# Moving a chunk's four row normalizations on ScalarE from positions 54–57 to 50–53 of a bidirectional Mamba kernel

## The chip, the cores and the metric

One core of a Trainium2 chip runs the whole program. The metric is the device time of one launch in microseconds. The kernel before was run three times; the median was 7565.02 us.

The engines are called as in the profile: PE (TensorE), DVE (VectorE), ACT (ScalarE), POOL (GpSimd) and SP (SyncE, which issues nearly all DMAs).

## The reference

The input is x, two sequences of 4096 rows of 512. The reference is a block with adaptive layer norms:

```
h = layernorm(x) * (1 + ca) + sa
x = x + ga * bidirectional_mamba(h)          # inner width 1024, 16 states per channel
h = layernorm(x) * (1 + cb) + sb
x = x + gb * fp6_quantized_linear(h)
```

The Mamba block projects h to u and z, runs a causal convolution of 4 taps and a SiLU over u, forms delta (a softplus), B and C from u, and then for each of 1024 channels and 16 states runs the recurrence

```
state[t] = exp(delta[t] * A) * state[t-1] + delta[t] * u[t] * B[t]
y[t]     = sum over the 16 states of state[t] * C[t]
```

followed by y + u*Dp, the gate silu(z), and an output projection. It runs once forwards and once backwards in time.

## The kernel before

The program has three parts: a short setup, the scan (from about 219 us to 7117 us of the profiled span), and a final stage with the second norm and the quantized linear. The change touches the scan alone.

The scan treats 32 chunks of 512 time steps: 16 forwards, 16 backwards. A chunk has 8 tiles of 128 channels (`MT`), and a tile has 16 states. Two states make one position, so a tile has 8 positions (`NQ`) and a chunk 64 (`POS`, p = 0 to 63). Every engine runs its own program, written out position by position, and they meet in semaphores. At each position:

- POOL multiplies B by delta*u for both states (`dBu`, L689). It works up to four pairs ahead of DVE. States 3, 4, 7 and 11 (`ASIDE`) are also multiplied by C on POOL (L698, tile `hR`), at the 6th position of the tile for 3 and 4, the 7th for 7 and the 8th for 11. Each of these waits until ACT has copied the last column of the state out of `hR` (L814, `aside_saved`), since the product overwrites it. At the 7th position POOL also makes delta and delta*u of the next tile (L672, L676).
- ACT makes exp(delta*A) for both states (L803) into a ring of four places in PSUM (`scans`), each free again when DVE has used the state from four before. Between these come its other duties: it empties PSUM banks (L740 the convolution into u, L751 z, L770 turned states, L759 B and C, L785 y), keeps states (L814), and at eight positions of the chunk (`GATED`) it switches to the SiLU table (L918), applies SiLU to u (L746) and z (L755), and switches back (L924).
- DVE runs the recurrence as a scan over 512 columns (L1160) and multiplies the other states by C (L1176, `hC`).
- PE adds the products up in PSUM (L1025) and does all projections, transposes and convolutions of this and the next chunk as background work (`SCHEDULE`).

Seven of the eight switches to SiLU stand at the last position of a tile (p = 7, 15, 23, 31, 39, 47, 63). The one of the seventh tile stands at p = 52, in the tile's middle, and does SiLU for two u tiles and z.

Rows of x for the chunk after the next are loaded into the first half of `comb` (`xin`) soon after p = 19 and are normalized in place by four ACT instructions of 128x512 (`normalize`, L791), one at each of the four positions from `NORM_POS` on, after the position's other duties and before its switch of tables if it has one. PE transposes them at p = 58, 60, 61 and 62 (`H0` to `H3`) and waits there for all four (`ln_done`).

Of the kernel before, what the change touches and what calls it, by code (L numbers as in the profile page):

```python
# [116 lines left out]
assert all(LAST[name][0][0] != "Y" for name in LAST if LAST[name][1])  # L117

RING = 2
NORM_POS = 54  # L120

# [234 lines left out]
def scan_stage(nc, io, dram):  # L358

    with ExitStack() as ctx:  # L360
# [345 lines left out]
        def _(act):  # L706
# [81 lines left out]
            def normalize(c, tt, table):  # L788
                if tt == 0:
                    act.wait_ge(x_loaded, c * (16 * TT) + 16 * TT)  # L790
                act.activation(xin[:, tt, :], xin[:, tt, :], ACT.Identity, scale=table[:, C_ROWS + tt:C_ROWS + tt + 1],  # L791
                               bias=table[:, C_ROWS + TT + tt:C_ROWS + TT + tt + 1]).then_inc(ln_done, 1)
# [59 lines left out]
            for i in range(CHUNKS):  # L852
# [4 lines left out]
                for j in range(MT):  # L857
# [3 lines left out]
                    for q in range(NQ):  # L861
# [52 lines left out]
                        for tt in range(TT):  # L914
                            if p == NORM_POS + tt:
                                normalize(i + 2, tt, cur)
# [709 lines left out]
```

## Time and profile before

| | us |
|---|---|
| median of three runs | 7565.02 |
| lowest and highest | 7552.77, 7570.42 |
| the profiled execution, its own time | 7552.77 |
| its span, first to last instruction | 7550.9 |
| PE, DVE, ACT, POOL busy in the span | 6864.3, 6824.4, 6159.4, 6964.4 |
| mean granted TensorE clock | 0.967 |

The busy times are sums over the whole span, setup and final stage included. Instructions on one engine overlap by some tens of nanoseconds, so what one costs in a queue is the distance between starts, not its duration. In a row of the timeline the bracket at the end gives the idle time before the instruction and who ended it; "issue" means that the profile shows no releaser.

### The profile page before, as it was taken

Reading aid. Unit: us, or ns where it says so; the run is one execution under the profiler, and the core shown is the slowest. Engines: PE = TensorE matmul, PEld = TensorE weight load, DVE = VectorE, ACT = ScalarE, POOL = GpSimd, SP = SyncE. Lnnn points to the kernel's source line nnn. Section 1 sums busy time; section 2 is a strip of 40 time slices with the busy share of each in tenths; the row PEclk is TensorE's granted clock in tenths of the full one; section 3 lists DMA queues with packets and bytes.
Section 4 is the critical chain, followed back from the end, with each engine's and each line's share of the span. In section 5 each row is a group of like instructions: output and inputs, shape, how many; then the busy total and the mean of one; then the engine's idle time right before and its main releaser. Section 6 shows DMA issues by size and latency. Waiting matters only on the chain. (4 is left out here: it accounts for less than half of the span.)

```text
span 7550.9 us, 110015 instructions
## 1 busy us (share of the span) xinstructions
PE 6864.3 (91%) x32682; PEld 4082.2 (54%) x32682; DVE 6824.4 (90%) x9069; ACT 6159.4 (82%) x12569; POOL 6964.4 (92%) x3774
## 2 busy tenths in 40 slices
PE   6899999999999999999999999999999999999889
PEld 3455555555555555555555555555555555555455
DVE  2799999999999999999999999999999999999766
ACT  1788888888888888888888888888888888888645
POOL 0899999999999999999999999999999999999678
PEclk8999999999999999999999999999999999999999
DMA  7544455444444454444444544444445444444555
GB/s 255 148 137 130 129 147 149 107 142 140 137 133 129 141 149 109 140 137 136 133 130 143 150 108 141 140 138 134 128 139 149 110 140 140 138 132 130 153 191 173
DMA packets 605392, 1064.01 MB, mean 141 GB/s; under 512 B 113584, under 2 KB 221872, under 8 KB 596336
## 3 DMA queue, kind: packets, MB, share of 16 engines
q1 hardware_dynamic: 602704, 1055.84, 47.7%
q8 instruction: 261, 4.28, 0.2%
q14 instruction: 347, 2.84, 0.1%
q10 hardware_dynamic: 2080, 1.05, 0.0%
HBM read 926.61 MB, written 130.05 MB: 140 GB/s over the span
## 5 line engine op out<-in xcount | busy, mean ns | idle before, releaser
L689 POOL TENSOR_TENSOR dBu<-Bb,du 128x1024 f32<-128x1024 f32 x2048 | 4784.6, 2365 | 1.9 <-DMA Bb<-bc_scratch 1.8
L1160 DVE TENSOR_TENSOR_SCAN scans<-scans,state,dBu 128x512 f32<-128x512 f32 x2304 | 2904.0, 1281 | 480.8 <-ACT scans L803 308.6
L803 ACT ACTIVATE scans<-delta,A 128x512 f32<-128x512 f32 x4096 | 2752.9, 693 | 356.0 <-DVE hC L1176 321.7
L1025 PE MATMUL yT<-ident,hC 128*128 128x128 f32 x9216 | 1411.7, 284 | 252.3 <-DVE hC L1176 250.0
L1176 DVE TENSOR_TENSOR hC<-scans,Cb 128x512 f32<-128x512 f32 x2304 | 1558.8, 682 | 0.0
L698 POOL TENSOR_TENSOR hR<-hR,Cb 128x512 f32<-128x512 f32 x1024 | 1293.7, 1275 | 220.8 <-ACT state L814 219.2
L1025 PEld LDWEIGHTS yT<-ident,hC 128*128 128x128 f32 x9216 | 1085.3, 145 | 654.0 <-DVE hC L1176 353.8
L1160 DVE TENSOR_TENSOR_SCAN hR<-scans,state,dBu 128x512 f32<-128x512 f32 x1024 | 1294.8, 1264 | 0.0
L1018 PE MATMUL bg<-u,comb 128*128 128x512 f32 x2112 | 989.1, 594 | 0.9 <-DVE u L1133 0.9
L1160 DVE TENSOR_TENSOR_SCAN hV<-scans,state,dBu 128x512 f32<-128x512 f32 x768 | 969.4, 1262 | 16.9 <-ACT scans L803 12.6
L957 PE MATMUL bg<-hT,win_u 128*128 128x512 f32 x2112 | 967.9, 599 | 0.9 <-ACT hT L725 0.9
L979 PE MATMUL bg<-hT,win_z 128*128 128x512 f32 x2048 | 963.5, 593 | 0.0
L770 ACT ACTIVATE turned<-bg,CT 128x128 f32<-128x128 f32 x3072 | 865.3, 365 | 42.1 <-PE bg L1002 38.2
L1025 PEld LDWEIGHTS yT<-ident,hR 128*128 128x128 f32 x4096 | 504.0, 151 | 363.3 <-issue 280.7
L1025 PE MATMUL yT<-ident,hR 128*128 128x128 f32 x4096 | 638.9, 293 | 59.9 <-POOL hR L698 59.9
L957 PEld LDWEIGHTS bg<-hT,win_u 128*128 128x128 f32 x2112 | 382.7, 191 | 445.0 <-issue 441.8
L1002 PEld LDWEIGHTS bg<-ident,hV 128*128 128x128 f32 x3072 | 374.7, 143 | 394.1 <-issue 254.3
L1018 PEld LDWEIGHTS bg<-u,comb 128*128 128x128 f32 x2112 | 368.6, 190 | 330.9 <-issue 323.4
L979 PEld LDWEIGHTS bg<-hT,win_z 128*128 128x128 f32 x2048 | 359.4, 191 | 306.0 <-issue 306.0
L1002 PE MATMUL bg<-ident,hV 128*128 128x128 f32 x3072 | 477.6, 279 | 50.8 <-DVE u L1133 30.0
L972 PE MATMUL bg<-comb,wtap 128*32 128x512 f32 x2080 | 299.3, 647 | 219.6 <-DMA comb<-pre_scratch 218.1
L1036 PEld LDWEIGHTS bg<-ident,turned 128*128 128x128 f32 x3084 | 366.5, 145 | 156.2 <-issue 156.2
(163 smaller groups left out, 7574.1 us busy)
## 6 DMA issues: line engine op xcount, KB each, us to landing
comb<-pre_scratch SPq DMA_DIRECT2D x1040, 256.0 KB, 4.6
Bb<-bc_scratch SPq DMA_DIRECT2D x264, 512.0 KB, 7.9
Cb<-bc_scratch SPq DMA_DIRECT2D x264, 512.0 KB, 8.6
win_u<-in_win SPq DMA_DIRECT2D x264, 256.0 KB, 4.7
pre_scratch<-pre SPq DMA_DIRECT2D x264, 256.0 KB, 3.8
comb<-comb_scratch SPq DMA_DIRECT2D x66, 1024.0 KB, 8.8
win_z<-in_win SPq DMA_DIRECT2D x257, 256.0 KB, 2.8
part_scratch<-pre SPq DMA_DIRECT2D x132, 256.0 KB, 2.0
```

Source lines behind the costliest of these rows:

```text
L689: pool.tensor_tensor(dBu[:, q % AHEAD], Bb[:, 2 * q:2 * q + 2, :], du[:, j % 2, :].unsqueeze(1).broadcast_to([P, 2, T]), ALU.mult).then_in ...
L698: pool.tensor_tensor(hR[:, k, :], hR[:, k, :], Cb[:, n, :], ALU.mult).then_inc(hR_made, 1)
L770: ins = act.mul(turned[:, TURNED.index(n), tt * P:(tt + 1) * P], bank[:, tt * P:(tt + 1) * P], CT[:, s, tt, n:n + 1])
L803: act.activation(place(n)[:], delta[:, j % 2, :], ACT.Exp, scale=A[:, i % 2, j * N + n:j * N + n + 1]).then_inc(dA_made, 1)
L957: ins = nc.tensor.matmul(bank[:], win_u[:, m % RING, k, :], hT[:, slot, k, :], start=(k == 0), stop=(k == KD - 1))
L979: ins = nc.tensor.matmul(bank[:], win_z[:, j % 2, k, :], hT[:, slot, k, :], start=(k == 0), stop=(k == KD - 1))
L1002: ins = nc.tensor.matmul(bank[:, tt * P:(tt + 1) * P], hV[:, TURNED.index(n), tt * P:(tt + 1) * P], ident[:], start=True, stop=True, is_tr ...
L1018: ins = nc.tensor.matmul(bank[:], comb[:, m, tt * P:(tt + 1) * P], u[:, s, m, :], start=(k == 0), stop=(k == MT - 1))
L1025: ins = nc.tensor.matmul(yT[:, tt * P:(tt + 1) * P], product[:, tt * P:(tt + 1) * P], ident[:], start=first and tt == 0, stop=False, is_tr ...
L1036: nc.tensor.matmul(bank[:, tt * P:(tt + 1) * P], turned[:, k, tt * P:(tt + 1) * P], ident[:], start=False, stop=False, is_transpose=True, ...
L1160: nc.vector.tensor_tensor_scan(to, place(n)[:], dBu[:, q % AHEAD, k, :], state[:, c:c + 1], ALU.mult, ALU.add).then_inc(h_made, 1)
L1176: nc.vector.tensor_tensor(hC[:, (j * NS + STRAIGHT.index(n)) % HC, :], bank[:], Cb[:, n, :], ALU.mult).then_inc(hC_made, 1)
```

## The change

One number: the position from which the four normalizations are issued.

```diff
-NORM_POS = 54
+NORM_POS = 50
```

It is read in one place, in ACT's loop over positions, `if p == NORM_POS + tt: normalize(i + 2, tt, cur)`. The programs of PE, DVE, POOL and SP are the same, instruction for instruction. On ACT two places differ, once in each of the 32 chunks.

ACT in the first chunk before, from the evacuation of the last convolution (p = 50) to the switch to SiLU (p = 52). L803 is the exponential, L721 the softplus's logarithm, L770 a turned state, L814 the copy of kept states, L751 z.

```order
L740 ACTIVATE u<-bg,bconv 128x512
L803 ACTIVATE scans<-delta,A 128x512
L721 ACTIVATE sp_a<-sp_a 128x512
L803 ACTIVATE scans<-delta,A 128x512
L770 ACTIVATE turned<-bg,CT 128x128 x4
L803 ACTIVATE scans<-delta,A 128x512
L814 COPY state<-hR 128x2
L751 COPY z<-bg 128x512
L803 ACTIVATE scans<-delta,A 128x512
L918 ACT_TABLE_LOAD
```

The same place in the changed kernel, where the last row here stands right ahead of the switch:

```order
L740 ACTIVATE u<-bg,bconv 128x512
L791 ACTIVATE comb<-comb,cur 128x512
L803 ACTIVATE scans<-delta,A 128x512
L721 ACTIVATE sp_a<-sp_a 128x512
L803 ACTIVATE scans<-delta,A 128x512
L770 ACTIVATE turned<-bg,CT 128x128 x4
L791 ACTIVATE comb<-comb,cur 128x512
L803 ACTIVATE scans<-delta,A 128x512
L814 COPY state<-hR 128x2
L751 COPY z<-bg 128x512
L803 ACTIVATE scans<-delta,A 128x512
L791 ACTIVATE comb<-comb,cur 128x512
```

Three L791 now stand ahead of the switch, one of them ahead of the copy L814 128x2 and two ahead of z.

The second place is on ACT too, from the return to the exponential's table (p = 52) to p = 55, before. The L814 128x1 at its head is the copy of state 7, the one at its end that of state 11.

```order
L924 ACT_TABLE_LOAD
L803 ACTIVATE scans<-delta,A 128x512 x2
L814 COPY state<-hR 128x1
L883 ACTIVATE state<-state,cur 128x16
L770 ACTIVATE turned<-bg,CT 128x128 x4
L803 ACTIVATE scans<-delta,A 128x512 x2
L814 COPY state<-hV 128x3
L791 ACTIVATE comb<-comb,cur 128x512
L803 ACTIVATE scans<-delta,A 128x512
L770 ACTIVATE turned<-bg,CT 128x128 x4
L803 ACTIVATE scans<-delta,A 128x512
L814 COPY state<-hR 128x1
```

The same in the changed kernel:

```order
L924 ACT_TABLE_LOAD
L803 ACTIVATE scans<-delta,A 128x512 x2
L814 COPY state<-hR 128x1
L883 ACTIVATE state<-state,cur 128x16
L770 ACTIVATE turned<-bg,CT 128x128 x4
L791 ACTIVATE comb<-comb,cur 128x512
L803 ACTIVATE scans<-delta,A 128x512 x2
L814 COPY state<-hV 128x3
L803 ACTIVATE scans<-delta,A 128x512
L770 ACTIVATE turned<-bg,CT 128x128 x4
L803 ACTIVATE scans<-delta,A 128x512
L814 COPY state<-hR 128x1
```

The fourth L791 stands one position earlier than the first one stood before, behind the copy of state 7 and ahead of two exponentials. The three that stood at p = 55, 56 and 57 are gone from there.

## Rows read from the trace of the kernel before

**Rows 1.** page: busy us of each engine, share of span, instructions
```profile
PE 6864.3 (91%) x32682; PEld 4082.2 (54%) x32682; DVE 6824.4 (90%) x9069; ACT 6159.4 (82%) x12569; POOL 6964.4 (92%) x3774
```

**Rows 2.** list of waits, POOL, whole span: us in total, times, longest
```profile
POOL hR L698 <- ACT state L814: 219.2, 162, 3.0
...
POOL dBu L689 <- DMA Bb<-bc_scratch: 1.8, 5, 0.7
```

**Rows 3.** windows: five of the eight tiles of chunk 8 (columns in the first row)
```profile
core 0: us, PE busy (x) PEld busy (x) DVE busy (x) ACT busy (x) POOL busy (x), PEclk, DMA share, GB/s
1940.03:1966.06 26.03, 23.02 (x101) 14.12 (x100) 25.36 (x34) 20.43 (x43) 25.95 (x14) 0.92 0.90 339
1966.06:1993.59 27.53, 27.53 (x131) 16.77 (x130) 26.09 (x34) 22.77 (x47) 26.09 (x15) 1.00 0.10 32
...
2045.81:2074.13 28.32, 26.18 (x137) 15.25 (x136) 26.30 (x35) 25.20 (x53) 26.06 (x15) 1.00 0.65 158
...
2101.49:2128.91 27.42, 23.77 (x128) 13.36 (x129) 24.38 (x33) 25.39 (x47) 26.03 (x14) 1.00 0.41 106
2128.91:2154.96 26.05, 21.10 (x115) 14.12 (x114) 25.84 (x34) 23.05 (x49) 25.97 (x14) 0.95 0.30 86
```

**Rows 4.** timeline of POOL, seventh tile of chunk 8: start us, us, what, [idle before]
```profile
2122.66 2.36 POOL L689 TENSOR_TENSOR dBu<-Bb,du 128x1024 f32<-128x1024 f32 x1
2126.34 1.27 POOL L698 TENSOR_TENSOR hR<-hR,Cb 128x512 f32<-128x512 f32 x1 [1.32 <-ACT state L814]
2127.56 1.28 POOL L672 TENSOR_TENSOR delta<-sp_a,sp_r 128x512 f32<-128x512 f32 x1
```

**Rows 5.** timeline of POOL, the same place in chunks 0 and 31
```profile
403.83 1.26 POOL L698 TENSOR_TENSOR hR<-hR,Cb 128x512 f32<-128x512 f32 x1 [1.31 <-ACT state L814]
...
7081.25 2.50 POOL L698 TENSOR_TENSOR hR<-hR,Cb 128x512 f32<-128x512 f32 x2 [0.35 <-ACT state L814]
...
7087.94 1.27 POOL L698 TENSOR_TENSOR hR<-hR,Cb 128x512 f32<-128x512 f32 x1 [1.89 <-ACT state L814]
```

**Rows 6.** timeline of ACT, chunk 8, positions 50 to 55
```profile
2114.25 0.68 ACT L740 ACTIVATE u<-bg,bconv 128x512 f32<-128x512 f32 x1
2115.99 0.69 ACT L803 ACTIVATE scans<-delta,A 128x512 f32<-128x512 f32 x1 [1.06 <-DVE hC L1176]
...
2119.92 0.72 ACT L803 ACTIVATE scans<-delta,A 128x512 f32<-128x512 f32 x1
2120.66 1.28 ACT L918 ACT_TABLE_LOAD   x1
...
2126.09 0.17 ACT L814 COPY state<-hR 128x1 f32<-128x1 f32 x1
...
2127.38 1.31 ACT L803 ACTIVATE scans<-delta,A 128x512 f32<-128x512 f32 x2
...
2128.69 0.83 ACT L791 ACTIVATE comb<-comb,cur 128x512 f32<-128x512 f32 x1
2129.40 0.68 ACT L803 ACTIVATE scans<-delta,A 128x512 f32<-128x512 f32 x1
```

**Rows 7.** groups of instructions, L791: count | busy us, mean ns | idle
```profile
L791 ACT ACTIVATE comb<-comb,cur 128x512 f32<-128x512 f32 x128 | 105.4, 824 | 0.0
```

**Rows 8.** timeline of DVE, the same stretch
```profile
2125.67 1.29 DVE L1160 TENSOR_TENSOR_SCAN scans<-scans,state,dBu 128x512 f32<-128x512 f32 x1 [1.33 <-ACT scans L803]
...
2128.69 2.46 DVE L1160 TENSOR_TENSOR_SCAN scans<-scans,state,dBu 128x512 f32<-128x512 f32 x2
...
2132.60 2.47 DVE L1160 TENSOR_TENSOR_SCAN scans<-scans,state,dBu 128x512 f32<-128x512 f32 x2 [0.21 <-issue]
```

**Rows 9.** timeline of PE, the same stretch
```profile
2124.39 0.66 PE L1025 MATMUL yT<-ident,hC 128*128 128x128 f32 x4 [1.33 <-DVE hC L1176]
```

**Rows 10.** windows of 3 us around the end of the eighth tile
```profile
2150.00:2153.00 3.00, 1.59 (x12) 1.60 (x13) 3.00 (x5) 3.00 (x10) 3.00 (x3) 0.90 0.01 4
2153.00:2156.00 3.00, 3.00 (x17) 3.00 (x16) 3.00 (x5) 2.77 (x8) 2.92 (x3) 0.54 0.28 59
```

## The prediction

> **What bounds the kernel now.** The page's busy times come first [rows 1]. Four engines are busy for 82 to 92% of the span, POOL most (6964.4 us), ACT least (6159.4 us). Such shares do not say which engine sets the end of a tile, so the next view is POOL's list of waits [rows 2]. In the scan it waits for one thing that matters: the product `hR` times C (L698) waits for ACT's copy of the state (L814), 219.2 us in 162 waits. For the loads of B it waits 1.8 us in all.
>
> The third view is the windows by tile [rows 3]. Each window runs on POOL from the start of one tile's delta*u (L676) to the start of the next, which lies one position and a half before the tile on the other engines. POOL's busy time is 25.95 to 26.09 us in every tile, whatever its length. So a tile lasts 26.0 us of POOL's work plus POOL's waits: 26.05 and 26.03 us in the eighth and the first tile, where it hardly waits, but 28.32 us in the fifth and 27.42 us in the seventh. Whatever makes POOL wait longer adds to the time, and whatever only fills other engines' idle time does not.
>
> The change lies in the seventh and eighth tile, so the fourth view is the timeline there. In chunk 8 POOL finishes its seventh pair at 2122.66 + 2.36 = 2125.02 us, and the product of state 7 starts only at 2126.34 us, 1.32 us idle [rows 4]. What it waited for is ACT's copy of state 7, issued at 2126.09 us, 0.17 us long [rows 6]. That copy stands behind the switch to SiLU at p = 52. This is so in all 32 chunks. There are 47 such waits in the seventh tiles; the first chunk's is 1.31 us and the last chunk's two are 0.35 and 1.89 us [rows 5], and together they make 67.0 us. In no chunk is POOL late enough for ACT to have slack at that copy. Behind the wait POOL runs on without a gap (L672 at 2127.56 us), and DVE, which waits 0.21 us for the pair of the tile's last position [rows 8], goes along with POOL.
>
> **What one normalization costs ACT.** It takes 824 ns in the mean, 128 times [rows 7], but instructions overlap: from the start of one at 2128.69 us to the start of the next instruction at 2129.40 us are 0.71 us [rows 6]. I take 0.71 us for each; the whole duration, 0.83 us, is the upper end.
>
> **The change part by part.** Nothing is added or removed; 4 x 32 = 128 instructions move. They issue no DMA, and no wait is new: the rows of x are loaded from p = 20 on, and `cur` is used at earlier positions already. The queues of SP, PE, DVE and POOL are as before.
>
> - First normalization, p = 50. It comes behind the evacuation of the convolution at 2114.25 us. The next exponential began at 2115.99 us, after ACT sat idle for 1.06 us waiting for DVE [rows 6]. 0.71 us fits into 1.06 us: cost 0. Without that cover it would be 0.71 us.
> - Second, p = 51, and third, p = 52. No idle time stands on ACT between 2115.99 us and the copy of state 7. Before the switch ACT runs into the table load without a gap: the exponential of 2119.92 us ends at 2120.64 us and the load begins at 2120.66 us [rows 6]. So both push the switch, the SiLUs and the copy of state 7 back by 2 x 0.71 = 1.42 us, and POOL, which already waits there, by as much. On the way the copy of states 3 and 4 is late by 0.71 us. A wait for it that this makes, like the 0.35 us of the last chunk, lies inside the 1.42 us, since POOL waits again behind it. DVE's wait for the first exponential after the switch, 1.33 us [rows 8], becomes 2.75 us by the same delay, not a further one. Cost 1.42 us per chunk; 2 x 0.83 = 1.66 us is the upper end.
> - Fourth, p = 53. It stands behind the copy of state 7, so POOL's wait does not see it, but ahead of the exponentials of p = 54. By the clock of the delayed engines these come 0.71 us later: the first ended at about 2127.38 + 0.69 = 2128.07 us, now at 2128.78 us, and DVE wants it at 2128.69 us [rows 6, 8]. That is 0.09 us late, or some 0.2 us with the time from one engine to the other (0.08 us from the end of ACT's copy, 2126.26 us, to POOL's start [rows 4, 6]). DVE has 0.21 us of waiting for POOL three scans later [rows 8]. I take 0; the ends are 0 and 0.71 us.
> - What is gone from p = 54 to 57. ACT saves there what it spent before. In the eighth tile ACT is busy for 23.05 of 26.05 us and in the first tile of the next chunk for 20.43 of 26.03 us, while POOL waits for nearly nothing (26.05 - 25.97 = 0.08 us, and 26.03 - 25.95 = 0.08 us) [rows 3]. The relief falls where ACT binds nobody. I take a gain of 0; the lower end is those 0.16 us per chunk.
>
> Sum: 2 x 0.71 x 32 = 45.4 us more. Against the profiled execution, 7552.8 us, that gives 7598 us. It is the lowest of three runs, 12 us under the median of 7565.0 us; carried to the median the sum is 7610 us, +0.60%. The ends of the terms: -0.16 x 32 = -5 us for the relief, and 0.24 x 32 = +8 us for full durations, 0.71 x 32 = +23 us each for the first and the fourth normalization.
>
> **The rivals.**
>
> *The stall is free.* ACT has 18% of idle time, and work moved about within its queue might find room. The time would stay at 7565 us. For it: ACT is the least busy of the four [rows 1]. Against it: in the 50 us around the change that idle time lies in the eighth and first tile, and the seventh has ACT at 25.39 of 27.42 us [rows 3], with the wait on its copy behind [rows 4]. The Trainium skill (Perfetto Trace Analysis, Identifying Performance Opportunities) says that improving a kernel generally means improving the engine with the highest occupancy. Read alone, that is POOL and not ACT, and the rule would price this change at 0. The rows above disagree for this stretch: POOL's gap ends with ACT. The same section also tells the reader to look at the gaps of that engine and what ends them, which is what was done here.
>
> *Given back in the second tile.* The other side. In the next chunk's second tile POOL's window is 27.53 us against 26.09 us busy, 1.44 us of waiting, and PE is busy in all of it [rows 3]: ACT waits there for PE, and POOL for ACT. If the B and C evacuation and the transposes of x, reached by ACT with three normalizations fewer ahead of them, let PE start the next chunk with less arrears, that wait could go: 1.44 x 32 = 46 us, and 45.4 - 46 = -0.7 us, 7564 us, not slower. It decides from the point where PE has no idle time left between the change and the second tile. Against it: PE idles 26.05 - 21.10 = 4.95 us in the eighth tile and 26.03 - 23.02 = 3.01 us in the first, so it has caught up by then, and starting its work earlier wins nothing.
>
> *More is exposed, or PE's clock falls.* If the first and the fourth normalization cost too, it is 4 x 0.71 x 32 = 90.9 us: 7656 us. Much the same comes from the clock. PE waits 1.33 us for DVE in the seventh tile [rows 9], which becomes 2.75 us. Late in the eighth tile, after PE was busy for 1.59 of 3 us, its granted clock is 0.54, near the lower level of 1.2 GHz [rows 10]. A window of 3 us at half speed loses 1.5 us of PE's work; were that on the chain in each chunk, it would be 48 us on top, 7658 us. Against it: the fourth has DVE's 0.21 us as cover, and PE has 4.95 us of idle time in the eighth tile to make good a fall.
>
> **How the numbers follow.** The forecast has 0.78, the free stall 0.05, the second tile 0.07, the greater cost 0.10. The predicted time is the forecast's, 7610 us; its own range is 7592 to 7635 us, from the ends above and some 8 us for the spread of the three runs. The range of 8 in 10 is 7585 to 7645 us: it takes in the half of the third rival in which one further normalization costs, and leaves out the two at about 7565 us, 0.12 together. A measurement of this kernel can tell 0.2%, 15 us, from no change. Faster by more needs the second tile's wait gone and part of the 45 us hidden: 0.03. Within it: 0.09. Slower: 0.88.
>
> **What would show it.** In the profile after, POOL's wait for L814 in the whole span is about 219 + 45 = 265 us; the seventh tile of chunk 8 lasts 28.8 us and not 27.4, while the other windows keep their lengths; ACT's idle time of 1.06 us before the exponential of p = 51 falls to 0.35 us; DVE's wait after the switch grows from 1.33 to 2.75 us; ACT's idle time in the eighth tile grows. A seventh tile of 27.4 us would make the forecast wrong in its main step. A second tile shorter than 27 us would show the second rival, and a seventh tile over 29.5 us, or a lengthened eighth, the third.

## The result and the profile after

The changed kernel is slower: 7640.28 us in the median of 4 runs (7634.85 to 7645.27) against 7561.79 us before. The ratio is 1.0104 with a 95% interval from 1.0087 to 1.0121, so about 78 us (66 to 91) were lost. The profiled execution of the changed kernel took 7615.2 us, with a span of 7613.5 us, and is faster than the median of its timed runs by some 25 us; its windows by tile show the smaller loss of about 62 us. The mean granted TensorE clock was 0.967 in the profile before and is 0.963 in this one, 0.959 to 0.961 in the four timed runs.

First the tiles of chunk 8 after, the columns as in [rows 3]: window, length, busy time of PE, PEld, DVE, ACT and POOL, PE's granted clock, and DMA.

```profile
1956.92:1983.17 26.25, 22.18 (x92) 13.60 (x91) 24.87 (x34) 20.30 (x42) 25.97 (x14) 0.87 0.88 327
1983.17:2011.08 27.91, 27.91 (x132) 16.91 (x131) 26.21 (x34) 22.74 (x47) 26.04 (x15) 1.00 0.11 32
...
2063.25:2091.27 28.02, 26.07 (x137) 15.16 (x136) 26.40 (x35) 25.02 (x53) 26.02 (x14) 1.00 0.65 161
...
2118.63:2148.80 30.17, 26.19 (x129) 15.42 (x130) 24.26 (x33) 27.50 (x49) 26.07 (x15) 0.89 0.38 97
2148.80:2175.30 26.50, 22.39 (x123) 14.81 (x122) 26.50 (x34) 20.87 (x48) 26.02 (x14) 0.94 0.32 92
```

These are the first, second, fifth, seventh and eighth tile. POOL is still busy for 26.0 us in each. The seventh grew from 27.42 to 30.17 us; some of this is chunk 8's own, since the mean over all 32 chunks went from 28.23 to 29.78 us. But the eighth has 26.50 us and not 26.05, the first 26.25 and not 26.03, and the second 27.91 and not 27.53. PE's clock over the first tile is 0.87, where it was 0.92.

Now ACT in the seventh tile after, answering to [rows 6]: start, duration, instruction, and in brackets the idle time before it.

```profile
2133.17 0.69 ACT L740 ACTIVATE u<-bg,bconv 128x512 f32<-128x512 f32 x1
2133.74 0.81 ACT L791 ACTIVATE comb<-comb,cur 128x512 f32<-128x512 f32 x1
2134.45 0.69 ACT L803 ACTIVATE scans<-delta,A 128x512 f32<-128x512 f32 x1
...
2137.19 0.84 ACT L791 ACTIVATE comb<-comb,cur 128x512 f32<-128x512 f32 x1
...
2139.69 0.83 ACT L791 ACTIVATE comb<-comb,cur 128x512 f32<-128x512 f32 x1
2140.55 1.28 ACT L918 ACT_TABLE_LOAD   x1
...
2145.97 0.17 ACT L814 COPY state<-hR 128x1 f32<-128x1 f32 x1
```

The first L791 follows the evacuation of 2133.17 us at once. In this chunk the exponential behind it has no idle time left ahead of it; in 19 of 32 chunks some 0.16 to 0.36 us are left of what was about 1 us. Two more L791 stand ahead of the table load. From the L791 of 2137.19 to the copy of state 7 at 2145.97 us ACT has no gap. Next POOL and DVE at that place, answering to [rows 4] and [rows 8]:

```profile
2138.80 2.50 POOL L698 TENSOR_TENSOR hR<-hR,Cb 128x512 f32<-128x512 f32 x2 [1.42 <-ACT state L814]
2141.26 2.36 POOL L689 TENSOR_TENSOR dBu<-Bb,du 128x1024 f32<-128x1024 f32 x1
2146.22 1.26 POOL L698 TENSOR_TENSOR hR<-hR,Cb 128x512 f32<-128x512 f32 x1 [2.60 <-ACT state L814]
```

```profile
2145.55 1.29 DVE L1160 TENSOR_TENSOR_SCAN scans<-scans,state,dBu 128x512 f32<-128x512 f32 x1 [2.81 <-ACT scans L803]
```

POOL's wait for the copy of state 7 is 2.60 us, and a wait of 1.42 us for the copy of states 3 and 4 stands ahead of it. DVE's wait for the exponential behind the switch went from 1.33 to 2.81 us. In the list of waits over the whole span (total, times, longest) these three answer to [rows 2] and to the forecast of 265 us for POOL's:

```profile
DVE scans L1160 <- ACT scans L803: 371.3, 246, 119.9
...
POOL hR L698 <- ACT state L814: 278.0, 211, 2.8
...
PE bg L1002 <- ACT turned L770: 66.8, 33, 2.2
```

POOL's was 219.2 us before. DVE's was 308.6 us and PE's wait for the turned state 20.3 us. DVE's longest, 119.9 us, is a single one that the kernel before has too (118.9 us). Inside the 32 seventh windows POOL's waits for this copy went from 67.0 to 115.4 us and DVE's for the exponentials from 71.4 to 127.3 us.

The last views show what the forecast did not contain: PE and its clock in the eighth tile and at the turn of the chunk. First PE's timeline, then windows of 3 us with the clock in the column before DMA's two, then ACT.

```profile
2147.43 0.66 PE L1002 MATMUL bg<-ident,hV 128*128 128x128 f32 x4 [2.11 <-ACT turned L770]
...
2156.85 1.92 PE L1031 MATMUL bg<-u,skip 128*128 128x512 f32 x2
2158.55 2.21 PE L1036 MATMUL bg<-ident,turned 128*128 128x128 f32 x12
...
2161.13 1.12 PE L1007 MATMUL bg<-dbc,wdt 32*128 32x512 f32 x2
```

```profile
2154.00:2157.00 3.00, 1.73 (x13) 1.26 (x11) 3.00 (x5) 0.69 (x1) 3.00 (x2) 0.94 0.00 0
2157.00:2160.00 3.00, 3.00 (x10) 1.86 (x9) 3.00 (x5) 1.91 (x4) 3.00 (x2) 0.50 0.00 0
2178.00:2181.00 3.00, 1.38 (x8) 0.75 (x8) 2.02 (x2) 2.96 (x4) 3.00 (x3) 0.92 1.01 384
2181.00:2184.00 3.00, 1.92 (x9) 1.92 (x10) 3.00 (x6) 1.87 (x3) 3.00 (x2) 0.50 1.02 415
2184.00:2187.00 3.00, 3.00 (x10) 1.86 (x9) 3.00 (x5) 2.42 (x4) 3.00 (x2) 0.50 1.03 418
```

```profile
2162.34 0.69 ACT L712 ACTIVATE sp_r<-bg,bdt 128x512 f32<-128x512 f32 x1 [1.77 <-issue]
```

The same instructions of chunk 8 in the kernel before:

```profile
2136.86 1.02 PE L1031 MATMUL bg<-u,skip 128*128 128x512 f32 x2
...
2139.56 1.12 PE L1007 MATMUL bg<-dbc,wdt 32*128 32x512 f32 x2
```

```profile
2140.76 0.69 ACT L712 ACTIVATE sp_r<-bg,bdt 128x512 f32<-128x512 f32 x1
```

PE waits 2.11 us at 2147.43 us. From 2157 us, at the head of the eighth tile, the granted clock is 0.50, that is 1.2 of 2.4 GHz, and the two instructions of the skip matmul (L1031) take 1.92 us where they took 1.02. Behind them comes the projection for the next delta (L1007), which starts 4.28 us after L1031 and not 2.70. ACT reads it in L712, and stood idle for 1.77 us before that. The profile names no releaser for this wait, but in both kernels L712 begins 0.08 to 0.09 us after L1007 has ended. In the mean over the 32 chunks ACT is idle for 1.06 us ahead of this L712, against 0.38 us before. The next fall is at 2181 to 2187 us, in the first tile. Before, in chunk 8, nothing fell at the head of the eighth tile, and the fall lay at its end [rows 10], with the window at 26.05 us all the same.

### The profile page after: what moved, and what is told of

Same layout as the page of the kernel before. It is cut to its first block and busy times, and to the rows that moved or that the text cites. A ratio compares the mean times of both kernels' runs of the same rounds, so it can differ in the third digit from the quotient of the medians.

```text
span 7613.5 us, 110015 instructions
## 1 busy us (share of the span) xinstructions
PE 6890.6 (91%) x32682; PEld 4090.0 (54%) x32682; DVE 6827.7 (90%) x9069; ACT 6158.4 (81%) x12569; POOL 6966.0 (91%) x3774
## 3 DMA queue, kind: packets, MB, share of 16 engines
q8 instruction: 261, 4.28, 0.2%
q14 instruction: 347, 2.84, 0.1%
## 5 line engine op out<-in xcount | busy, mean ns | idle before, releaser
L803 ACT ACTIVATE scans<-delta,A 128x512 f32<-128x512 f32 x4096 | 2757.2, 694 | 395.8 <-DVE hC L1176 317.9
L770 ACT ACTIVATE turned<-bg,CT 128x128 f32<-128x128 f32 x3072 | 866.8, 367 | 39.8 <-PE bg L1002 36.0
L1002 PE MATMUL bg<-ident,hV 128*128 128x128 f32 x3072 | 472.6, 277 | 92.5 <-ACT turned L770 66.8
L1036 PEld LDWEIGHTS bg<-ident,turned 128*128 128x128 f32 x3084 | 387.9, 151 | 164.8 <-issue 164.8
```

The source lines that it names most:

```text
L770: ins = act.mul(turned[:, TURNED.index(n), tt * P:(tt + 1) * P], bank[:, tt * P:(tt + 1) * P], CT[:, s, tt, n:n + 1])
L803: act.activation(place(n)[:], delta[:, j % 2, :], ACT.Exp, scale=A[:, i % 2, j * N + n:j * N + n + 1]).then_inc(dA_made, 1)
L1002: ins = nc.tensor.matmul(bank[:, tt * P:(tt + 1) * P], hV[:, TURNED.index(n), tt * P:(tt + 1) * P], ident[:], start=True, stop=True, is_tr ...
L1036: nc.tensor.matmul(bank[:, tt * P:(tt + 1) * P], turned[:, k, tt * P:(tt + 1) * P], ident[:], start=False, stop=False, is_transpose=True, ...
```

## The experiments

Each was timed beside the kernel before. Ratios are to the kernel before, with 95% intervals; where the difference of the medians says something else, both are given. Windows by tile run from one L676 on POOL to the next, as in [rows 3], and their means are over the 32 chunks of one profile. `NORM_AT` lists the positions of the four normalizations, `if p == NORM_AT[tt]` reads it; before it is (54, 55, 56, 57), after (50, 51, 52, 53).

### Which of the four costs

**Only the first moved.**

```diff
-NORM_AT = (54, 55, 56, 57)
+NORM_AT = (50, 55, 56, 57)
```

> Only the first normalization moved from p = 54 to p = 50, the others at 55, 56 and 57 as before. Theory (only what stands between p = 50 and the copy of state 7 and finds no idle time on ACT costs): 0, within 0.1% of before, since it falls into ACT's idle 1.06 us. Rival (the 33 us that the change costs beyond 2 x 0.71 x 32 = 45 us come from the first and fourth normalization being exposed in part): 10 to 23 us slower.

Measured: 7563.48 us, ratio 1.0003 (0.9994 to 1.0012). Free, as the idle time before the next exponential said.

**Only the fourth.**

```diff
+NORM_AT = (53, 55, 56, 57)
```

> One normalization at p = 53, behind the copy of state 7, the others at 55, 56 and 57. Theory: 0 to 5 us slower, since POOL's wait does not see it. Rival (exponentials of p = 54 late for DVE): up to 23 us slower.

Measured: 7559.25 us, ratio 0.9996 (0.9987 to 1.0005). Free too. Both values at 0 in the sum hold, each taken alone.

**The two in the middle.**

```diff
+NORM_AT = (51, 52, 56, 57)
```

> Two normalizations ahead of the switch, at p = 51 and 52, the other two at 56 and 57 as before. Theory of exposure alone: 45 us slower (0.6%), the change's other 33 us missing. Theory with the clock (the longer wait of PE in the seventh tile moves PE's clock falls to where they cost): 60 to 78 us slower, nearly all of the change's loss.

Measured: 7631.82 us, ratio 1.0091 (1.0077 to 1.0105), 69 us. Two normalizations carry nearly the whole loss of the change, and more than the 45 us of their own time. In the windows of all 32 chunks the seventh tile is 1.41 us longer than with the first alone moved (29.84 against 28.43 us in the mean), which is the 2 x 0.71 us of the sum, 45 us. Against the kernel before, 28.23 us, it is 1.61 us. The mean of this window differs that much between profiles in which nothing, or only the first, was added ahead of the switch: it lies between 28.08 and 28.46 us in the six of them, so some 6 us of the sum over the chunks can't be told. The eighth, first and second are longer than with the first alone by 0.19, 0.10 and 0.26 us, together 0.55 x 32 = 18 us.

**One, and four.**

```diff
+NORM_AT = (51, 55, 56, 57)     # one ahead of the switch
+NORM_AT = (51, 51, 52, 52)     # four ahead of it
```

> One normalization ahead of the switch, at p = 51, the others at 55, 56 and 57. Theory: 0.71 x 32 = 23 us slower by the exponentials behind the switch, plus 0 to 15 us by where PE's clock falls. If the loss were linear through the change's 78 us for two, it would be 39 us.

> All four between the idle time and the switch: two at p = 51, two at p = 52. Theory: POOL's wait for the copy of state 7 grows by 4 x 0.71 = 2.84 us in each of 32 chunks, 91 us, plus the clock's share, if there is one, of 15 to 60 us. Rival (POOL and DVE have slack somewhere behind): less than 91 us, sub-linear against the change.

Measured: one 7589.57 us, ratio 1.0034 (1.0022 to 1.0046), 26 us by the ratio and 33 us in the medians; four 7659.74 us, ratio 1.0125 (1.0110 to 1.0141), 95 us. The seventh tile has 29.03 us with one, 31.30 us with four, against 28.23 us before: 0.80 and 3.07 us more, near 0.71 and 2.84 us. So the part in the seventh tile is in proportion to the work ahead of the switch. The rest is not: 3 us by the ratio or 10 us by the medians for one, 24 us for the middle two, 4 us for four. The six runs with one ahead spread from 7571.97 us at a granted clock of 0.971 to 7593.78 us at 0.965, the slower the lower the clock; so time and clock go together within one and the same kernel too.

### Through which wait it costs

**The copy of state 7 ahead of the switch,** in the kernel before and in the changed one. The copy then lies at the end of the fifth position of every tile, in the seventh right before the table load.

```diff
-                    if n != ns[-1] + 4:
+                    if n != (COPY_7 if ns == (7,) else ns[-1] + 4):
                         continue
...
+                        if q == 4:
+                            keep_states(g, j, COPY_7)
                         if p in GATED:
```

> The kernel before, with ACT's copy of state 7 taken from its place behind the exponential of state 11 to the end of the tile's fifth position, in the seventh tile thus ahead of the switch to SiLU. Theory (POOL's wait for this copy sets the length of tiles 2, 5, 6 and 7): POOL no longer waits there, and the time falls by at least 67 us if nothing takes its place; DVE's wait of 1.33 us for the exponentials after the switch is the next limit, so I expect 20 to 100 us faster. Rival (DVE, which waits for ACT behind the switch by as much, is the true bound and POOL's wait only mirrors it): no change, within 0.2%.

> The changed kernel (all four normalizations at p = 50 to 53), with the same early copy of state 7. Theory (the change costs only by that copy): within 15 us of the kernel before with the early copy. Rival (DVE's wait for the exponentials behind the switch, 2.75 us instead of 1.33, binds as well): 45 us or more slower than it.

Measured: on the kernel before 7555.63 us, ratio 0.9994 (0.9985 to 1.0003), no change; on the changed one 7626.31 us, ratio 1.0094 (1.0081 to 1.0108). The 20 to 100 us gain did not come, and the loss stayed. POOL and DVE in chunk 8 of the first of these show why:

```profile
2128.60 1.27 POOL L699 TENSOR_TENSOR hR<-hR,Cb 128x512 f32<-128x512 f32 x1
...
2135.68 1.28 POOL L699 TENSOR_TENSOR hR<-hR,Cb 128x512 f32<-128x512 f32 x1 [0.93 <-ACT state L815]
```

```profile
2129.53 1.29 DVE L1163 TENSOR_TENSOR_SCAN scans<-scans,state,dBu 128x512 f32<-128x512 f32 x1 [1.59 <-ACT scans L804]
```

POOL's product of state 7, at 2128.60 us, waits no more. One position later the product of state 11 waits 0.93 us for its own copy, which hangs on the same ACT queue behind the switch, and DVE waits 1.59 us for the exponential. The mean lengths of the seventh and eighth window add up to 26.33 + 27.64 = 53.97 us, against 28.23 + 26.09 = 54.32 us before. POOL's waits for ACT did not go, they moved: in the seventh and eighth windows together they are 54 us, against 68 us before, and 121.4 us with the early copy in the changed kernel, against 122.5 us without it. DVE's there are 80 us, against 71 us before. So the copy of state 7 was the first place to show ACT's delay, and not the only way in which it costs. Whether the next copy or the exponentials for DVE bind in its place was not taken apart.

### Whether it is PE

**Idle matmuls in one of PE's waits, and in three.** Both on the changed kernel, into a bank that is empty, and overwritten later; the second has the first and these:

```diff
+                        if kind == "T" and p == 53:
+                            pe.wait_ge(bg_free, freed(i, "Z6"))
+                            for _ in range(3):
+                                nc.tensor.matmul(bg[1][:], win_z[:, 0, 0, :], hT[:, s, 0, :], start=True, stop=True)
...
+                                if (j, n) in ((6, 8), (6, 14)):     # second kernel only
+                                    pe.wait_ge(bg_free, freed(i, "Z6"))
+                                    for _ in range(2):
+                                        nc.tensor.matmul(bg[1][:], win_z[:, 0, 0, :], hT[:, s, 0, :], start=True, stop=True)
                                 pe.wait_ge(hC_made, straight(g, n + 1))
```

> The changed kernel, with three idle matmuls of 128x512 on PE at p = 53 of each chunk, into a bank that is empty there, where PE otherwise waits for ACT's evacuation of a turned state (2.08 us per chunk). Their results are overwritten. Theory with the clock (the 20 to 30 us beyond 45 come from PE's clock falling after this wait): the eighth tile's 26.5 us and the second's 27.9 us get rarer, 10 to 30 us faster than the changed kernel, to about 7615 us. Rival (the clock's falls are a symptom): no change, or some us slower.

> The changed kernel with seven idle matmuls of 128x512 on PE per chunk, 3.4 us, laid into three of its waits in the seventh tile (two while it waits for the product of state 8, three for the turned state, two for the product of state 14), into an empty bank. Theory (PE's idle time in the seventh tile makes its clock fall in the eighth and first tile, which costs what the change costs beyond 45 us): the fall in the eighth tile goes, its windows of 26.5 us become 26.0, and the time is 8 to 33 us under the changed kernel. Rival (it was not the idle time of the seventh tile): as the changed kernel, 7640 us, or more.

Measured: with one wait filled 7636.92 us, ratio 1.0106 (1.0090 to 1.0121), as the changed kernel. With three filled 7603.82 us, ratio 1.0056 (1.0042 to 1.0070), 42 us over the kernel before by the ratio and 47 us by the medians. Its interval lies wholly under that of the change (1.0087 to 1.0121), both taken against the kernel before beside which each ran. Seven matmuls per chunk that compute nothing took back 0.48%, some 36 us, with the two intervals some 20 to 53 us. What the change had cost beyond 45 us is 33 us. The trace shows the seven as 14 instructions, busy for 6.6 us per chunk, and not for the 3.4 us expected. The same filling was not run on the kernel before, so part of the gain might be had there too. Its eighth and first windows, 26.09 and 26.02 us in the mean, leave nearly nothing to win above POOL's 26.0 us of work; its second, at 27.30 us, might. The seventh and eighth tile of chunk 8:

```profile
2125.19:2154.56 29.37, 27.94 (x128) 15.82 (x129) 24.23 (x33) 27.60 (x49) 26.11 (x15) 0.94 0.41 102
2154.56:2180.62 26.06, 22.49 (x133) 15.19 (x132) 26.06 (x34) 21.04 (x47) 25.98 (x14) 1.00 0.32 91
```

The eighth is back at 26.06 us with the clock at 1.00 over it. No eighth window of this kernel is over 26.4 us; of the changed one, 16 of 32 are. ACT's idle time ahead of L712 in the eighth tile is 0.12 us in the mean, where it was 1.06 us. In the means of the two profiles the eighth, first and second tile are 0.22, 0.10 and 0.29 us shorter than in the changed kernel, 20 us over the chunks; the seventh is the same, 29.78 us. The profiles in whole differ by only 5 us, as that of the changed kernel was faster than its median and this one slower.

**The windows of all chunks.** A chunk in which PE's clock over the first tile is under 0.9 has a longer second tile in every kernel but one, that in which PE alone waits longer (below). Read from the windows of each profile; the two with the early copy are left out, since their eighth windows start elsewhere:

| kernel | first tiles with clock under 0.9 | second tile after these | after the others | eighth tiles over 26.4 us |
|---|---|---|---|---|
| before | 2 of 32 | 27.92 us | 27.26 us | 2 |
| first only | 4 | 27.91 | 27.24 | 4 |
| fourth only | 8 | 27.78 | 27.30 | 4 |
| one ahead | 11 | 27.82 | 27.24 | 6 |
| middle two | 22 | 27.86 | 26.96 | 16 |
| after | 20 | 27.83 | 27.01 | 16 |
| after, one wait filled | 24 | 27.86 | 27.33 | 18 |
| after, three filled | 13 | 27.83 | 26.82 | 0 |
| four ahead | 4 | 27.68 | 27.29 | 0 |
| PE alone waits | 2 | 27.04 | 27.21 | 0 |
| extra work in the eighth | 4 | 27.64 | 26.89 | 2 |
| in the fourth tile | 7 | 27.67 | 27.25 | 3 |

For the eighth tile the place of the fall decides. The twelve kernels have 384 eighth windows. In all 71 of them over 26.4 us the granted clock was at half for some time between 5 and 14 us after the window's start. In 34 others it was so too, and in the 279 in which it was not, none is over 26.10 us. Such a fall stands in 7 of 32 chunks before, in 19 of the changed kernel, and in none with three waits filled or with PE alone waiting.

With four ahead the falls come earlier, in 30 of 32 chunks within 4 us of the window's start, in chunk 8 at 2160 us:

```profile
2160.00:2163.00 3.00, 3.00 (x12) 1.80 (x11) 3.00 (x4) 2.75 (x9) 2.92 (x3) 0.53 0.00 0
```

The mean clock over the eighth tile is 0.897 there and its length 26.05 us, with 0.17 us of idle time on ACT ahead of L712. At that place they cost nothing that the window shows, and that kernel loses its 91 us and hardly more, though its granted clock, 0.960 in the profile, is as low as that of the changed kernel.

**PE alone waits longer,** in the kernel before.

```diff
+                        if kind == "T" and p == 53:
+                            pe.wait_ge(dA_made, (i * MT + 6) * N + 14 + DU0)
```

> The kernel before, in which PE alone waits longer: at p = 53 it waits until ACT has done the exponential of state 13, some 1.2 us beyond the 0.64 us that it waits there for the turned state; no other engine is changed. Theory with the clock: the seventh tile keeps its 28.2 us, while the eighth, first and second lengthen as in the changed kernel, 10 to 33 us slower. Rival (PE has slack, its later start and its clock cost nothing): no change.

Measured: 7555.12 us, ratio 0.9994 (0.9985 to 1.0003). The wait was there, with 20.3 us before in its place and 66.8 us in the changed kernel:

```profile
PE bg L1002 <- ACT scans L803: 58.4, 32, 1.8
```

It cost nothing, and the clock over the eighth tile was 0.945, no lower than the 0.932 before. So this one wait of PE is not sufficient to bring the falls of the changed kernel. That it takes ACT's and DVE's delay with it, by which PE's other waits stand differently too, is a reading that no run tests.

**Extra work at the end of the eighth tile,** before. The transposes of `H2` are done four times over.

```diff
+                            if k == 2:
+                                for _ in range(3):
+                                    for tt in range(TT):
+                                        nc.tensor.matmul(bank[:, tt * P:(tt + 1) * P], xin[:, tt, k * P:(k + 1) * P], ident[:],
+                                                         start=True, stop=True, is_transpose=True, skip_group_check=True)
                             transpose_x(bank, k, i + 2)
```

> The kernel before, with the four transposes of H2 (p = 61, late in the eighth tile) done four times over, same values, where PE waits 1.92 us for DVE. Theory with the clock: the fall at the end of the eighth tile (0.54 in 3 us) goes, the second tile gets shorter than 27.3 us, 0 to 35 us faster. Rival (falls there cost nothing): no change.

Measured: 7571.03 us, ratio 1.0014 (1.0005 to 1.0023). The second tile did shorten, from 27.30 to 26.98 us in the mean, but the first grew from 26.02 to 26.61 us, and ACT waits 62 us in the first tiles for PE's transposes of x, where it waited for none of them before. On the clock it says nothing: the falls at the end of the eighth tile did not go, with 96 us at half the clock there over all chunks, against 99 us before.

### Another place

**The four normalizations in the fourth tile.**

```diff
+NORM_AT = (26, 27, 28, 29)
```

> The four normalizations at p = 26 to 29, in the fourth tile, where ACT sits idle 3.6 us per chunk waiting for PE and POOL waits for ACT only 0.2 us. Theory (only ACT's work between p = 50 and the exponentials behind the switch costs): no change, within 10 us. Rival (a normalization costs its 0.71 us wherever ACT is ahead of DVE by little): 23 to 91 us slower.

Measured: 7572.69 us, ratio 1.0020 (1.0011 to 1.0029), 16 us slower. The fourth tile grew from 26.29 to 26.96 us, 0.67 x 32 = 21 us, as much as one of the four normalizations. It shows in POOL's waits for ACT's copies in that tile, 26.4 us against 4.6. ACT's idle time in this tile, most of it for PE, did not hide all of the work. No version of these was faster than the kernel before by more than its interval.

## Why the prediction was right, and where it fell short

- *The sign, the range and the main term held.* 7640 us lies within 7585 to 7645 us, near its upper end, and outside the forecast's own range of 7592 to 7635 us. The sum's term, 2 x 0.71 x 32 = 45.4 us, is shown: the middle two alone lengthen the seventh tile by 1.41 us, and with three of PE's waits filled the changed kernel is 42 to 47 us over the kernel before. The loss is 78 us, so the sum missed two fifths of it. That it still lies in the range is partly luck: the range was widened upward for the first or the fourth normalization, and both cost 0; what filled the room was the clock.
- *First normalization, cost 0; fourth, cost 0.* Shown, each alone.
- *By its own signs the third rival came as well.* A seventh tile of chunk 8 over 29.5 us or a lengthened eighth was to show it; they have 30.17 and 26.50 us. POOL's waits for the copies are 278 us and not 265. DVE's wait behind the switch is 2.81 us, near the 2.75 us forecast.
- *The relief at p = 54 to 57, gain 0.* ACT's idle time in the eighth tile grew (20.87 of 26.50 us busy in chunk 8, against 23.05 of 26.05 us [rows 3]) and no window got shorter for it.
- *The wait for the copy of state 7 was too narrow a path.* The step took this copy as the way in which ACT's delay reaches the end. Taken out of the way it changed nothing, in either kernel. The delay also reaches DVE through the exponentials behind the switch, which the prediction named and set beside it ("by the same delay, not a further one"), and POOL through the copy of state 11. With the wait for the first copy gone, these two were left, and the time stayed. "Whatever makes POOL wait longer adds to the time" still stands: POOL's waits in the two tiles were as long in sum with the early copy in the changed kernel, and so was the time. The size was right because all of these hang on the same ACT queue.
- *Two readings of rows were off.* DVE's 0.21 us [rows 8] has "issue" as its releaser and not POOL, so it was no proof of cover for the fourth normalization, which cost nothing all the same. And the ends that the sum lists upward, 8, 23 and 23 us, are more than the 25 us by which its own range goes up.
- *The mis-sized term is PE's clock.* It stood at 0 in the sum, with 48 us in the third rival and the argument that PE's 4.95 us of idle time in the eighth tile could "make good a fall". What is left of the 78 us beyond 45 is about 33 us, and filling PE's waits took 36 us off. The windows of the profiles place some 20 us of it, 0.20, 0.20 and 0.22 us in the eighth, first and second tile. Idle time in the eighth tile did not help, because the fall came near the tile's head, ahead of the projection that ACT waits for. PE's wait for DVE, which was to grow from 1.33 to 2.75 us, did not: 37 us in all seventh tiles before, 31 us after. It was the wait for the turned state that grew, from 20.3 to 66.8 us.
- *The second rival,* a shorter second tile, did not come; that tile went from 27.30 to 27.52 us in the mean. *The free stall* fell with the middle two.
- *Open:* which of PE's waits decide where the clock falls. Filling one, or lengthening one, left the time as it was; filling three did not. Whether the idle matmuls act by the clock alone was not tried apart. For the second tile the table shows that it goes with the clock over the first, and not that the clock is the cause.

The rule of the Trainium skill that the prediction weighed (Perfetto Trace Analysis, Identifying Performance Opportunities), read alone, would have priced the change at 0. The runs say 78 us for work of the least busy engine, in a stretch in which it has no gap.

## What to carry to other kernels

Work moved within a queue is priced by the stretch that it enters: count the instructions between the last idle time and what others wait for, each by the distance between starts, and what finds idle time ahead costs nothing. Then ask where the other engines' new idle time falls, since a PE that has waited may come back at half its clock just ahead of something that is waited for. And when one wait seems to set the pace, take away its cause before believing it: several engines may be waiting for the same queue.

## What was not expected of the hardware

Matmuls that compute nothing made a kernel some 36 us faster: seven per chunk, 6.6 us of PE's time, at three of PE's waits. In the profile after, the clock stood at 0.50 for 3 us at the head of the eighth tile and for 6 us in the first, and a first tile with a mean clock under 0.9 was followed by a second tile of 27.8 us in the changed kernel, 27.0 us otherwise. Over the kernels of the table that difference lies between 0.4 and 1.0 us, but for the one in which PE alone waits (-0.2 us, with two such chunks). PE idles 4.3 us in the seventh window in the mean (3.2 us before) and 4.3 us in the eighth (4.8 us before), and the place of a fall mattered more than this idle time: with four ahead, at a clock of 0.960, the falls cost next to nothing, and in the changed kernel, at 0.959 to 0.961, about 33 us.
